# A gated delta-rule recurrence in fp32: squares summed first, step operations on all 16 rows, small copies moved off VectorE

## The reference, cut to what matters

```python
def step(state, inp):
    r_t, k_t, v_t, w_t, a_t, kk_t = inp
    sa = einsum('bhij,bhj->bhi', state, -kk_t)
    state = w_t[..., None] * state + sa[..., None] * (kk_t * a_t)[:, :, None, :] \
            + k_t[..., None] * v_t[:, :, None, :]
    norm = sqrt(mean(state * state, axis=-1, keepdims=True))
    state = state / (norm + EPS_STATE)
    o_t = sum(state * r_t[..., None], axis=-1)
    return (state, o_t)
...
out = g * out @ Wo.T
nrm = sqrt(mean(out * out, axis=-1, keepdims=True))
out = x_g + out / (nrm + EPS_RMS) * ln_weight       # x_g = x + 0.1 * conv(x)
```

## Time and profile before

| | |
|---|---|
| median of 3 runs | 2437.0 us (2434.69 to 2437.7) |
| the profiled execution, own time | 2441.28 us |
| its span, first to last instruction | 2439.2 us |
| VectorE (DVE) busy | 2187.4 us, 90% |
| TensorE (PE) busy | 1925.3 us, 79% |
| ScalarE (ACT) busy | 1585.6 us, 65% |
| GpSimd (POOL) busy | 903.2 us, 37% |
| recurrence, first step to last | 725 to 2257 us of the span |

### The profile page before, as it was taken

The page is one execution under the profiler, slowest core; times in us unless marked ns, Lnnn a source line. Parts: engine busy times, 40 slices in busy tenths (PEclk is TensorE's granted clock), DMA queues, the critical chain, the costliest instruction groups (busy, mean ns, idle before and its releaser), DMA issues.

```text
span 2439.2 us, 47897 instructions
## 1 busy us (share of the span) xinstructions
PE 1925.3 (79%) x12321; PEld 1556.6 (64%) x12321; DVE 2187.4 (90%) x8800; ACT 1585.6 (65%) x5168; POOL 903.2 (37%) x1528
## 2 busy tenths in 40 slices
PE   5888888788888878888888878688887877344787
PEld 3555555455687867777777767677777767343555
DVE  6888887689619999999999999999999999999887
ACT  4878888577646665666666666666666565444776
POOL 0000000011105555555555555555555555555110
PEclk8999999699977787787877777987778777655899
DMA  5000000000000000000000000000000000000011
GB/s 183 17 17 22 17 21 23 3 1 1 1 1 1 1 1 1 1 1 1 1 1 1 1 1 1 1 1 1 1 1 1 1 1 1 1 1 1 1 35 35
DMA packets 14353, 25.02 MB, mean 10 GB/s; under 512 B 1280, under 2 KB 12032, under 8 KB 13824
## 3 DMA queue, kind: packets, MB, share of 16 engines
q1 hardware_dynamic: 14080, 21.97, 3.0%
HBM read 12.27 MB, written 4.19 MB: 7 GB/s over the span
## 4 chain that ended last, share of the span: by engine, by line
DVE 57%; issue 16%; PE 15%; ACT 6%; POOL 0%; DVEq 0%; POOLq 0%; ACTq 0%
DVE pn L1563 11%; DVE bank L1579 10%; DVE U L1620 8%; DVE xs L1551 5%; DVE bank L1568 5%; DVE kv L1612 4%; PE bank L282 3%; PE bank L267 2%; ACT prob L923 2%; PE bank L585 2%; DVE bank L1609 1%; PE bank L761 1%; DVE bank L1588 1%; DVE bank L1532 1%; PE bank L632 1%
## 5 line engine op out<-in xcount | busy, mean ns | idle before, releaser
L1748 POOL TENSOR_TENSOR wu<-U,stg 128x256 f32<-128x256 f32 x512 | 318.6, 622 | 682.2 <-DVE U L1620 682.2
L750 PE MATMUL bank<-U,ident 128*128 128x128 f32 x2048 | 464.2, 399 | 81.6 <-ACT go L1064 69.3
L750 PEld LDWEIGHTS bank<-U,ident 128*128 128x128 f32 x2048 | 426.7, 238 | 121.5 <-issue 90.6
L761 PE MATMUL bank<-stack,tm 128*128 128x64 f32 x1792 | 336.4, 374 | 145.7 <-ACT tm L994 137.2
L1213 ACT ACTIVATE xs<-U 128x128 f32<-128x128 f32 x1024 | 261.5, 302 | 275.5 <-DVE U L1620 271.6
L761 PEld LDWEIGHTS bank<-stack,tm 128*128 128x128 f32 x1792 | 325.6, 284 | 162.9 <-ACT tm L994 153.0
L1563 DVE TENSOR_REDUCE pn<-xs 128x16 f32<-128x256 f32 x1024 | 377.6, 408 | 0.6 <-issue 0.2
L1701 POOL TENSOR_TENSOR kv<-stg 128x256 f32<-128x256 f32 x513 | 318.7, 621 | 0.0
L1131 ACT ACTIVATE small<-pn 128x16 f32<-128x16 f32 x513 | 110.9, 216 | 295.0 <-DVE pn L1563 295.0
L735 PE MATMUL bank<-wcat,yT 128*128 128x224 f32 x1024 | 294.6, 447 | 2.5 <-issue 2.0
L1579 DVE TENSOR_TENSOR bank<-wu,bank 128x128 f32<-128x128 f32 x1024 | 292.0, 285 | 1.1 <-POOL wu L1748 0.8
(11 more groups left out here) (214 smaller groups left out, 3567.6 us busy)
## 6 DMA issues: line engine op xcount, KB each, us to landing
out_x<-x SPq DMA_DIRECT2D x8, 512.0 KB, 2.9
x<-in_x SPq DMA_DIRECT2D x1, 3584.0 KB, 17.7
Vs<-V SPq DMA_DIRECT2D x8, 384.0 KB, 4.6
Vs<-V SPq DMA_DIRECT2D x8, 288.0 KB, 3.3
lane<-in_lanes SPq DMA_DIRECT2D x8, 256.0 KB, 3.2
wcat<-in_wcat SPq DMA_DIRECT2D x1, 1792.0 KB, 13.2
wraw<-in_w_up SPq DMA_DIRECT2D x1, 1024.0 KB, 19.6
wraw<-in_w_down SPq DMA_DIRECT2D x1, 1024.0 KB, 11.4
```

Source lines behind the costliest of these rows:

```text
L750: last = pe.matmul(rsum.rearrange("p (t i) -> p t i", i=HD), ident[:, :], steps[:, :, :, j], start=(j == 0), stop=(j == HD - 1))
L761: last = pe.matmul(bank[3 + g][:, e * CH:(e + 1) * CH], tm[:, g * (PB // 2) + e, :, :].rearrange("p a c -> p (a c)"), stack[:, :], start=T ...
L1748: pool.tensor_tensor(ij(wu[:, :]), ij(U[:, half if j else 1 - half, (j - 1) % STEPS, :]), col(stg[:, half, j, TW, :]), ALU.mult).then_inc( ...
```

## The change

In a step:

- The square sums get a reduction of their own over both halves, placed ahead of the product sums; `root` on ScalarE waits for this one alone (`S["ps"]`). The product sums are one reduction over both halves.
- z is one operation of 256 elements, and so is kv (at `jj != 3`). p, d, the lam product and U stay in halves.
- The scale sg stands ahead of d, and kv between the two halves of d.
- VectorE's copies of kk rows and of the ring are gone. ScalarE copies kk of four steps (`copy_kk`, L1103), kk*a of four steps (`copy_kka`, L1107) into two new places of bank 0, and takes the logarithm of the ring straight from PSUM, 64 elements twice in a batch (`log_norms`, L1135). Each stands behind the squares and waits (`beside_sums`) for both p of the next step; VectorE's z waits for each of them (at `jj` = 1, 2, 3).
- The convolution is copied out by ScalarE (`evacuate_convolution`, L1090) and added by GpSimd; an output tile is scaled by ScalarE (`scale_outputs`), weighted and added by GpSimd (`weigh_output`, `add_output`). VectorE keeps two operations on one column.
- ScalarE's side work moves: `factors` and `retention(1)` ahead of the squares, `evacuate_outputs` to the next batch's first step, `gates(1)` to `j` = 7.

```diff
-                            if jj == 1:
-                                dve.wait_ge(S["sg"], t0 + j)
-                                if g == 0:
-                                    dve.tensor_copy(hist[:, 1 - half, RENORM:, :], sring).then_inc(S["h"], 1)
...
+                            square_sums(t0 + j)
                             for e in range(2):
                                 dve.wait_ge(T[e]["x"], t1)
-                                dve.wait_ge(T[e]["sq"], t0 + j)
-                                dve.tensor_reduce(pn[:, e, :, :].rearrange("p a i -> p (a i)"),
-                                                  xs[:, e, :, :].rearrange("p a (i j) -> p (a i) j", j=HD), AXX,
-                                                  ALU.add).then_inc(T[e]["pn"], 1)
-                            for e in range(2):
-                                dve.wait_ge(T[e]["pn"], t1)
-                                dve.tensor_tensor(ij(rows8(zz, e)), col(pn[:, e, 0, :], HD // 2),
-                                                  row(kkz[:, jj, 1, :], i=HD // 2), ALU.mult).then_inc(T[e]["z"], 1)
+                            dve.tensor_reduce(pn[:, :, 0, :], xs[:, :, 0, :].rearrange("p e (i j) -> p e i j", j=HD), AXX,
+                                              ALU.add).then_inc(S["pn"], 1)
+                            if jj == 1:
+                                dve.wait_ge(G["ls"], it * 2 + (g + 1))
+                            if jj == 2:
+                                dve.wait_ge(S["ka"], it * 2 + (g + 2))
+                            if jj == 3:
+                                dve.wait_ge(S["kk"], it * 2 + (g + 2))
+                            dve.wait_ge(S["pn"], t1)
+                            dve.tensor_tensor(zz.rearrange("p (e i j) -> p e i j", e=2, j=HD),
+                                              pn[:, :, 0, :].unsqueeze(3).to_broadcast([P, 2, HD // 2, HD]),
+                                              kkar[:, g, jj, :].unsqueeze(1).unsqueeze(1).to_broadcast([P, 2, HD // 2, HD]),
+                                              ALU.mult).then_inc(S["z"], 1)
...
+            def square_sums(t):
+                for e in range(2):
+                    dve.wait_ge(T[e]["sq"], t)
+                dve.tensor_reduce(pn[:, :, 1, :], xs[:, :, 1, :].rearrange("p e (i j) -> p e i j", j=HD), AXX,
+                                  ALU.add).then_inc(S["ps"], 1)
...
             def root(t1):
-                for e in range(2):
-                    act.wait_ge(T[e]["pn"], t1)
+                act.wait_ge(S["ps"], t1)
...
+            def beside_sums(t1):
+                for e in range(2):
+                    act.wait_ge(T[e]["x"], t1)
...
+            def add_convolution(n, m):
...
+                pool.wait_ge(C["x1"], (TURN[yt] * B + m) * 2 + 1)
+                xt = x[:, m * NT + yt, :]
+                pool.tensor_tensor(xt, xt, otmp, ALU.add).then_inc(C["x1"], 1)
```

More of the change, by code:

```diff
@@ L54 @@
 QKK, QW, QKKA, QK, QV, QR, QG = range(7)
-TKK, TKKA, TW, TK, TV = range(5)
+TKKA, TW, TK, TV = range(4)
 E_MAX = 1e18
@@ L216, in build @@
         S = {n: sem("s_" + n) for n in (
-            "ln rt sg lam kk h wu k0 rsum rse").split()}
-        T = [{n: sem(f"t{e}_" + n) for n in "u x sq pn z d k".split()} for e in range(2)]
-        G = {n: sem("g_" + n) for n in "kk kv e1 wd e2 wc ka g1 gm g2 f1 ls f2 fc".split()}
+            "ln rt sg lam kk ka k ps pn z wu k0 rsum rse").split()}
+        T = [{n: sem(f"t{e}_" + n) for n in "u x sq d".split()} for e in range(2)]
+        G = {n: sem("g_" + n) for n in "kv e1 wd e2 wc ka g1 gm g2 f1 ls f2 fc".split()}
         O = {n: sem("o_" + n) for n in "ov os t1 t1c gs gt gc pr sq ln sd dn rs t x".split()}
@@ L1188, in _ @@
                         for j in range(STEPS):
-                            root(t0 + (j + 1))
+                            t1 = t0 + (j + 1)
+                            jj, g = j % RENORM, j // RENORM
+                            root(t1)
                             if j == 0:
+                                if m >= 1:
+                                    evacuate_outputs(n, m - 1)
+                                elif n >= 1:
+                                    evacuate_outputs(n - 1, NB - 1)
                                 normalise(n, m)
+                                if m == 0 and ot is not None:
+                                    act.wait_ge(O["t1c"], (2 * ot + 2) * NB)
                                 stage_batch(n, m)
                             if j == 1:
-                                act.wait_ge(G["wc"], it + 1)
+                                if n + 1 < NCH:
+                                    act.wait_ge(C["rc"], (n + 1) * NB * 2 - 2 + 2 * m)
+                                else:
+                                    act.wait_ge(C["rc"], NCH * NB * 2)
                                 gates(0, it, row_it)
@@ L1231, in _ @@
-                            if j == 7:
-                                evacuate_outputs(n, m)
+                            if t1 < L and (j + 1) % RENORM == 1:
+                                beside_sums(t1 + 1)
+                                act.wait_ge(S["sg"], t1)
+                                act.wait_ge(G["f2"], it + (j + 1) // RENORM)
+                                log_norms(0 if j + 1 > RENORM else 1)
+                            if t1 < L and (j + 1) % RENORM == 2:
+                                beside_sums(t1 + 1)
+                                if t1 > RENORM:
+                                    act.wait_ge(S["z"], t1 - 2)
+                                act.wait_ge(G["ka"], it + 1 + g)
+                                copy_kka(half if g == 0 else 1 - half, 1 - g)
@@ L1233, in _ @@
+                            if t1 < L and (j + 1) % RENORM == 3:
+                                beside_sums(t1 + 1)
+                                copy_kk(row_it + RENORM if g == 0 else row_next)
             root(L + 1)
-            log_norms(L // STEPS, 1, L // RENORM + 1)
+            act.wait_ge(S["sg"], L + 1)
+            log_norms(1)
             factors(L // STEPS, 1)
+            evacuate_outputs(NCH - 1, NB - 1)
             act.wait_ge(O["ov"], L // STEPS + 1)
@@ L1622, in _ @@
             dve.wait_ge(S["rt"], L)
-            for e in range(2):
-                dve.wait_ge(T[e]["sq"], L)
-                dve.tensor_reduce(pn[:, e, 1, :], ij(xs[:, e, 1, :]), AXX, ALU.add).then_inc(T[e]["pn"], 1)
+            square_sums(L)
             dve.wait_ge(O["ov"], L // STEPS)
```

219 lines of the change are left out of this document (112 added, 107 removed).

## The result

The changed kernel takes 2496.7 us (2495.41 to 2498.45, 4 runs) against 2436.3 us before on the same chip: a ratio of 1.0249, 95% interval 1.0231 to 1.0266. It is 60 us slower where 71 us less were forecast.

A forecast was written before the change was run, and what follows sets the result against it. VectorE was taken to bound the recurrence; 34.6 us from steps (mostly copies), 24 from output work, 1 from small operations and 11 from late squares sum to 71, so 2437.0 - 71 = 2366 us, range 2350 to 2398.

The forecast's parts named there:

- The step that failed: Dependent instructions in the recurrence: start 0.04 us after the one just before ends, read from the earlier trace.
- One of the signs that I had named: On VectorE: the prediction is wrong if z starts later than 0.04 behind its sums.
- The rest of the sum: Whole kernel: forecast 2366 us, from 2437.0 less a saving of 71 us.
- the price I took for the wide operations: 256-element VectorE operations: 0.41 us each, for z taken from another 256-element operation with a PSUM operand.
- the term that I had put on late squares: Steps whose squares wait for ScalarE's side work, as at j = 4: 11 us that would go.
- the step's sum: Plain step: 2.80 us before, 2.79 after; fusing and reordering save 0.21 and added dependences give back 0.20.
- The output work: Convolution additions and output tiles leaving VectorE: 28.1 us, less 4 that covered the root's wait, bringing 24 us.
- The 0.065 saved for each fused pair: z and kv on VectorE: one 256-element instruction instead of two halves saves 0.065 us each; said to agree with 60 ns on SBUF.
- The kk copy's worth: VectorE's kk copy at jj = 3: costs 0.18 us, counted as saved by its removal.
- ScalarE did not become the bound: Loaded steps: ScalarE becomes the bound, squares 0.12 late in five steps of eight, costing 38 us, 2404; chance 0.12.
- the second rival: z waits for ScalarE's copies in 6 steps of 8, making the kernel slower, 2454 us; chance 0.04.
- GpSimd's added reads: Moved work on GpSimd: its reads hold VectorE, 50 us at most, 2416; chance 0.03.

The follow-up runs named there:

- the three orders turned: Changed kernel with wait order turned on VectorE at square reduction (second square first), z (sums before copy) and first d (z before wu): 2398.9 us, ratio 0.9837.
- the halved step with the same care for waits: Changed kernel with the earlier step in halves, new copies and additions kept, and waits reordered at root, jj = 0 first product and reductions: 2363.5 us, ratio 0.9716.
- moves only: Changed kernel with the step itself as before, in halves; ScalarE's and GpSimd's new copies and additions kept: 2398.9 us, ratio 0.9841.
- kernel with the root's waits turned: Kernel before the change, only the order of the root's two waits on ScalarE turned, second half's sums named first: 2414.0 us, ratio 0.9915.

## Why the prediction was wrong

**The step that failed** is "An instruction that reads what the one just before it wrote starts 0.04 after its end", used for every dependence in the new step. It was measured at an instruction with one wait; the 0.03 behind the squares came from the scale, which has two waits but carries the later one itself. The three dependences that the change puts on the path belong to instructions with two waits (z in six steps of eight), the later one in the separate instruction. Each cost 0.065 us more than I gave it: 0.065 x (512 + 512 + 384) = 92 us, and 98 us by measurement. That turned a gain into a loss. One of the signs that I had named for the prediction being wrong, z starting later than 0.04 behind its sums, came true. The clue was in the earlier trace rows: I read that the logarithm starts 0.09 after the reduction, and wrote it down as what ScalarE takes, though the exponential right behind it, with one wait, starts 0.03 after the logarithm. The root has two waits. I carried the 0.09 into the new step as well; there it has one wait and took 0.04 (1508.56, 1508.60). And the waits of each instruction stood in the listed streams.

**The rest of the sum** was 2366, and with the three orders turned the kernel takes 2399. Of these 33 us, some 23 are in the lengths of the steps: the median plain step of that kernel takes 2.84 instead of 2.79, and at jj = 3 it takes 3.08 instead of 3.03. z and the square reduction, at 0.43 and 0.42 instead of 0.41, and the spacings behind them account for it; so the price I took for the wide operations was a little low. The other 11 us are the term that I had put on late squares, and that was wrong. In the kernel before, the squares are late in 54 of 64 steps with j = 5, but the ring's copy runs meanwhile, and the step takes 2.93 like that with j = 1, whose squares are on time. In the kernel with the three orders turned no squares are late, and 11 us of time above the median step are there all the same, in single steps; what causes them stays open.

**Right, by the step's own points.** The squares end 0.43 into the step, as forecast. The root no longer sets the start of the scale: the exponential ends ahead of it. In the step shown the copy (L1135) ends at 1508.39, well before z's sums at 1508.89. Fusing gains nothing over halves, as the step's sum said, even with the three orders turned; the halved step with the same care for waits is even 35 us faster (2363.5 against 2398.9, of which some 4 us are the order at jj = 0, which the fused kernel did not get). The late squares behind the side work of j = 4 are gone in the changed kernel, though they cost less than I thought. The output work brought what I forecast: per batch, j = 6 and 7 took 0.36 us more than j = 2 and 3 before (means), 23 us in all, and with the moves only they take the same. The 0.065 saved for each fused pair is there too (spacings of 0.34 instead of twice 0.20). But both pairs, z and kv, have an operand in PSUM, so their agreement with a figure for SBUF, which the prediction claims, says nothing about that figure.

**Wrong in size.** The kk copy's worth, as shown by the run of moves only, 0.07 instead of 0.18: I subtracted its full spacing and did not ask what it covered. In the changed kernel itself the second d stands in its place, so there the removal counted in full.

**The rivals.** ScalarE did not become the bound: the squares are on time in every step of the changed kernel. z did wait where the second rival said, "in 6 steps of 8", and at the instruction it named, but not for the copy's end; the mere presence of the copy's semaphore moved the sums' wait into the separate instruction. That rival's sign was right and its mechanism wrong. GpSimd's added reads cost nothing that a run shows: the moves, with ScalarE's part, are a gain of 39 us, and the output work's share came in full. On this the Trainium skill's warning (Perfetto Trace Analysis, Optimizing Scalar/DVE Operations), that moving work between GpSimd and VectorE might not help, is not borne out by this kernel, in which no VectorE instruction of the new steps reads both inputs from SBUF.

## What to carry to other kernels

Where an instruction waits for several semaphores, name first the one that comes last. In kernels built like this one the instruction itself then carries it. No run shows a cost of this, and it was worth 24 us of 2437 in the old kernel and 98 us in the new one. Before fusing instructions of a chain bound by one engine, add up the dependences that the fusing lays bare, at the price of the wait they really have, and not the instructions saved. Before removing an instruction, ask which latency it filled.

## What was not expected of the hardware

- A release of a waiting instruction takes 0.035 us when the instruction carries the wait, and 0.10 us when the wait is a separate instruction ahead of it. That is VectorE; on ScalarE it is 0.03 and 0.09 (kernel with the root's waits turned, and before). The Trainium skill (VectorE: DVE Perf Modes, The DRAIN you can't avoid) says that a semaphore after each of a row of copies costs nothing extra. That is about signalling; no run here tests it. A second wait on one instruction, where it is the one that comes last, is not free: 98 us in 1408 places are 0.07 us each.
- At jj = 0 the first p has three waits, of which U comes last. Naming U first brought p some 0.02 us forward in the traces, not the 0.04 expected; the 5 us of which this is a part stay unproved by themselves.
- The first step of the recurrence began between 713 and 726 us in the profiled executions of these kernels. Two of them, at 713 and 714, differ from the kernel before, at 725, only in the order of two waits inside the steps. Spans compare less well than the recurrence itself.
